# A tangent computed by an exponential and three VectorE steps in the first router of a fused decoder layer

## The reference

```python
pooled = x.mean(axis=1)
h = jnp.tanh(pooled @ W1 + b1)            # 64 values
logits = h @ W2 + b2                      # 8 experts
probs = jax.nn.softmax(logits, axis=-1)
top_p, top_i = jax.lax.top_k(probs, 3)    # top_w = top_p / sum
# x + sum over the three experts of  w * (gelu(x @ Wa[e]) @ Wb[e])
```

## Time and profile before

| | us |
|---|---|
| median of 3 runs | 1166.26 |
| lowest, highest | 1164.23, 1167.35 |
| the profiled execution | 1166.95 |
| its span, first to last instruction | 1165.2 |
| TensorE busy | 1112.1 (95%) |
| VectorE busy | 896.5 (77%) |
| ScalarE busy | 815.4 (70%) |
| GpSimd busy | 576.3 (49%) |
| mean granted TensorE clock | 0.986 of full |

### The profile page before, as it was taken

How to read it: one execution, slowest core, us unless ns; L and a number is a source line. 1 busy time by engine, 2 the same in 40 slices (tenths; PEclk the granted TensorE clock), 3 DMA queues, 4 the chain that set the end, 5 groups by cost and what they waited for, 6 DMA issues and landing times.

```text
span 1165.2 us, 24724 instructions
## 1 busy us (share of the span) xinstructions
PE 1112.1 (95%) x8375; PEld 516.4 (44%) x8375; DVE 896.5 (77%) x2816; ACT 815.4 (70%) x1553; POOL 576.3 (49%) x594
## 2 busy tenths in 40 slices
PE   7799999999999999978999999999989999999998
PEld 3344444444444444335422223233223676666666
DVE  4678888888788878875999988998975768565654
ACT  5467767766666666654588897887886867657563
POOL 2878888888888888856324344443312130000000
PEclk9899999999999999998999999999998999999999
DMA  7744333343333333104223131221205324234200
GB/s 215 212 131 120 88 111 88 87 120 82 84 91 85 86 86 86 51 1 113 57 58 83 57 83 55 74 65 48 64 1 188 103 73 145 91 106 130 73 19 19
DMA packets 81859, 102.86 MB, mean 88 GB/s; under 512 B 11875, under 2 KB 73571, under 8 KB 81735
## 3 DMA queue, kind: packets, MB, share of 16 engines
q1 hardware_dynamic: 81574, 100.90, 29.9%
q10 hardware_dynamic: 160, 0.39, 0.2%
HBM read 65.27 MB, written 10.68 MB: 65 GB/s over the span
## 4 chain that ended last, share of the span: by engine, by line
PE 40%; DVE 6%; ACT 5%; issue 4%; ACTq 0%
PE a_s L1534 11%; PE a_m L1520 7%; PE a_o L1453 7%; PE a_m L1403 4%; DVE a_mx L1875 3%; PE a_s L1433 3%; PE a_a L169 3%; PE a_s L1520 2%; ACT a_pt L1678 2%; PE a_s L169 1%; PE a_a L1461 1%; ACT a_osb L1684 1%; PE a_m L1478 0%; DVE a_mx L1872 0%; ACT a_back L1690 0%
## 5 line engine op out<-in xcount | busy, mean ns | idle before, releaser
L1678 ACT ACTIVATE a_pt<-a_s 128x512 f32<-128x512 f32 (+1 forms) x448 | 228.8, 574 | 50.5 <-PE a_s L1433 47.7
L739 ACT ACTIVATE a_pt<-a_s 128x512 f32<-128x512 f32 x256 | 152.9, 598 | 130.0 <-DVE a_s L893 126.1
L1875 DVE TENSOR_REDUCE a_mx<-a_m 128x1 f32<-128x512 f32 x256 | 163.0, 683 | 21.0 <-PE a_m L1403 20.2
L884 DVE CUSTOM_DVE_ANT_0 a_junk<-a_m,a_rtile 128x512 f16<-128x512 f32 x256 | 167.2, 686 | 0.5 <-issue 0.5
L996 POOL TENSOR_TENSOR a_ps<-a_ps,a_pt 128x512 f32<-128x512 f32 x126 | 159.8, 1290 | 3.2 <-ACT a_pt L739 3.1
L893 DVE TENSOR_TENSOR a_s<-a_s,a_near 128x218 f32<-128x218 f32 (+1 forms) x256 | 108.0, 432 | 41.8 <-PE a_s L527 41.8
L538 PE MATMUL a_o<-a_pt,a_v 128*64 128x512 f32 x512 | 124.0, 605 | 0.0
L1872 DVE CUSTOM_DVE_ANT_0 a_junk<-a_m,a_causal 128x512 f16<-128x512 f32 (+3 forms) x256 | 113.8, 486 | 6.2 <-issue 5.8
L526 PE MATMUL a_s<-a_q,a_k 128*128 128x512 f16 x256 | 98.5, 385 | 5.7 <-ACT a_pt L739 5.6
L1008 POOL TENSOR_TENSOR x_acc<-x_acc,a_part 128x256 f32<-128x256 f32 x120 | 87.3, 728 | 27.2 <-DVE x_acc L916 26.4
L527 PE MATMUL a_s<-a_q,a_k 74*128 74x512 f16 x256 | 98.5, 385 | 0.0
(11 more groups left out here) (328 smaller groups left out, 2633.6 us busy)
## 6 DMA issues: line engine op xcount, KB each, us to landing
a_rtile<-lines SPq DMA_DIRECT2D x32, 448.0 KB, 3.9
a_q<-a_nat SPq DMA_DIRECT2D x192, 64.0 KB
a_k<-a_nat SPq DMA_DIRECT2D x192, 64.0 KB
a_vy<-in_Wa SPq DMA_DIRECT2D x12, 1024.0 KB, 5.0
a_vy<-in_Wb SPq DMA_DIRECT2D x12, 1024.0 KB, 7.5
a_qk<-halves SPq DMA_DIRECT2D x40, 128.0 KB, 2.8
halves<-a_held SPq DMA_DIRECT2D x16, 256.0 KB, 2.2
halves<-a_held SPq DMA_DIRECT2D x32, 128.0 KB, 2.4
```

Source lines behind the costliest of these rows:

```text
L739: act.activation(pt[:, n % RING, ::-1], bank_s[j % 2][:, :], ACT.Exp, scale=SC1 / QS).then_inc(sm["act_s"], 1)
L884: dve.tensor_tensor_reduce(junk[h][:, :], bank_m[h][:, :], rtile[:, u % 3, h, qb * P:qb * P + S], -1 / MAXROW, 3e38, ALU.add, ALU.min, mx[ ...
L1678: act.activation(to, frm, ACT.Exp, scale=SC2 / QS).then_inc(sm["act_s"], 1)
L1875: dve.tensor_reduce(mx[u % 2][:, qb, to:to + 1], frm, AX.X, ALU.max).then_inc(sm["dve_b"], 1)
```

## The change

In the router of batches 0 and 1 the Tanh is replaced by tanh(z) = 1 - 2 / (exp(2z) + 1). VectorE adds the bias and bounds z at 40 (`bounded`, step 240), ScalarE takes exp(2z) (step 241, where Tanh stood at the end of step 240), and VectorE adds 1, inverts, and multiplies by -2 and adds 1 into `ht` (`tangent`, step 241). The second product moves from step 241 to 243 on TensorE, with the VectorE and ScalarE parts behind it from step 242 to 244, the spread from 245 to 246, and `wbc` and `chosen` from 246 to 247. The router of batches 2 and 3 keeps its Tanh.

```diff
-        rt = semaphores(nc, ctx, "rt", "ld one pe act v")
+        rt = semaphores(nc, ctx, "rt", "ld one pe act v tangent")
+        hz, he = sb("hz", [RH, 2]), sb("he", [RH, 2])
-        POOLED, FIRST, SECOND, SPREAD, SPLIT0, UP0 = 236, 240, 241, 245, 254, 265
+        POOLED, FIRST, SECOND, SPREAD, SPLIT0, UP0 = 236, 240, 243, 246, 254, 265
@@ TensorE, route, part 1
                     pe.wait_ge(rt["act"], 3 * r + 2)
+                    if r == 0:
+                        pe.wait_ge(rt["tangent"], 4)
@@ ScalarE, route
+                elif part == 1 and r == 0:
+                    act.wait_ge(rt["tangent"], 1)
+                    act.activation(he[:, :], hz[:, :], ACT.Exp, scale=2.0).then_inc(rt["act"], 1)
                 elif part == 1:
                     act.wait_ge(rt["pe"], 3 * r + 1)
-                    if r == 0:
-                        act.wait_ge(rt["ld"], len(loads) * DMA)
@@ ScalarE, clock
-                for i, at in enumerate((POOLED, FIRST, SECOND + 1)):
+                for i, at in enumerate((POOLED, FIRST + 1, SECOND + 1)):
@@ VectorE
+            def bounded(frm):
+                dve.wait_ge(rt["pe"], 1)
+                dve.wait_ge(rt["ld"], len(loads) * DMA)
+                dve.tensor_scalar(hz[:, :], frm[0:RH, 16:18], b1[:, :], 40.0, ALU.add, ALU.min).then_inc(rt["tangent"], 1)
+            def tangent():
+                dve.wait_ge(rt["act"], 2)
+                dve.tensor_scalar(he[:, :], he[:, :], 1.0, None, ALU.add).then_inc(rt["tangent"], 1)
+                dve.wait_ge(rt["tangent"], 2)
+                dve.reciprocal(hz[:, :], he[:, :]).then_inc(rt["tangent"], 1)
+                dve.wait_ge(rt["tangent"], 3)
+                dve.tensor_scalar(ht[0:RH, 0:2], hz[:, :], -2.0, 1.0, ALU.mult, ALU.add).then_inc(rt["tangent"], 1)
@@ VectorE, clock
+                if n == FIRST:
+                    bounded(bank_m[0])
+                if n == FIRST + 1:
+                    tangent()
```

## The result

| | before | after |
|---|---|---|
| median | 1166.68 us (11 runs) | 1162.58 us (11 runs) |
| lowest, highest | 1164.23, 1167.48 | 1160.67, 1164.27 |
| span of the profiled execution | 1165.2 | 1162.1 |
| mean granted clock in it | 0.986 | 0.992 |

The ratio of after to before is 0.997, with a 95% interval of 0.996 to 0.9981: the changed kernel is 4.1 us faster in the medians. 1161.6 us was forecast.

What follows compares the result with a forecast made beforehand. TensorE, busy 95%, was taken to bound the kernel, losing time to a 1.36 us gap and the half-speed clock behind it. Removing 4.7 us (1.36 - 0.5 gap, 3.8 clock) from 1166.26 gave 1161.6 us, range 1159.5 to 1166.0.

Steps and rivals of the forecast that it cites:

- TensorE's gain of 4.7 us in the tail: From 868.6 us to the products with values behind the spread: 1.36 - 0.5 of gap plus 3.8 of clock.
- its slack: Choice of experts ends near 878.2 on VectorE, TensorE reaches the spread at 879.0: 0.8 us, so no wait.
- The four steps: VectorE's bound, add, invert and multiply-add: 0.2 us each, the first hidden, the other three 0.6 us before the second product.
- No table load: The Exp replacing Tanh on ScalarE needs no load, so the Tanh's load of 1.28 us goes.
- The drain: The skill adds about 1.38 us to ScalarE's 1.28 us load; the prediction expected no such drain to be saved.
- The slack behind the experts' weights: Last transposition waiting for `weigh_last`: 3.7 us of slack shrinks to 0.7 us, so the gain is narrowly not capped.
- 1.7 us earlier: Experts' loads issued once `chosen` ends, at 880.0 against 881.76: 1.7 us earlier, while TensorE comes 4.7 us earlier.
- Does the clock hold: Clock stays 1.00 around 870 us because the fall looks narrow and about 0.9 us leaves the gap; 3.8 us rests on it.
- the table load stays: Rival: the load stays ahead of the new Exp and stalls a score bank, gap 1.1 us; 1166 us, chance 0.03.
- the wait moves to the spread: Rival: VectorE's chain ends late, TensorE waits 1.4 us at step 246, clock falls; 1167.5 us, up to 1170, chance 0.08.

Runs made afterwards that it cites:

- the gap filled over 128 rows: Kernel before with six idle products over all 128 rows on TensorE ahead of the second product; 1166.3 us, and 1165.33 us when run again.
- the kernel with the load forced back: Changed kernel with a table load (exp_and_others) forced ahead of the new exponential; 1166.97 us, ratio 0.9998.
- the move alone: Kernel before with the second product at step 243 and the spread at 246, Tanh and its table load kept; 1166.97 us, ratio 1.0.
- the kernel with the long gap and no load: Changed kernel with second product at step 241, spread at 245, ScalarE's exponential still at the end of step 241; 1167.74 us, ratio 1.0.
- idle products over 64 rows: Kernel before with six idle products (64x128 weights, 512 columns) on TensorE ahead of the second product; 1164.71 us, ratio 0.9992.

## Why the prediction was right, point by point

- **TensorE's gain of 4.7 us in the tail**: measured 4.78 (16.99 - 12.21), and 281.22 us behind it in both. The profiles of another kernel agree with the split: the gap filled over 128 rows gives 3.66 us for the clock (forecast 3.8), and the rest, 4.78 - 3.66 = 1.1, is the gap's (0.9). The medians of that kernel, 0.6 and 1.5 us below the kernel before, do not confirm it.
- **Positions**, each less the 1.68 us of different start: tangent ready 870.60 (forecast 870.8), choice of experts 878.05 (878.2), spread 878.89 (879.0), its slack 0.84 (0.8), `chosen` 879.70 (880.0).
- **The four steps**: 0.16 to 0.21 us each, 0.2 from one start to the next, as taken. The new Exp: 0.20.
- **No table load**: right. From 560 to 900 us the preload is the only one left:

```profile
L1772 ACT ACT_TABLE_LOAD x1 | 1.3, 1283 | 0.0
```

- **The drain** that the Trainium skill, "ScalarE: Activation LUTs", section "What ACT_TABLE_LOAD costs", adds to the load: not seen. Where the load was forced back, it started 0.02 us after the exponentials ahead of it ended (871.54, 871.56), and the next activation came 1.30 us after its start.
- **The slack behind the experts' weights** was mis-sized: forecast 0.7 us, measured 2.4 (`weigh_last` ends at 898.79, the transposition starts at 901.21). Its term "1.7 us earlier" is 3.5 after the different start (900.63 - 898.79 + 1.68): `chosen` is 0.3 us earlier than I had it, from there to the first split it takes 6.36 us against 7.08, and the four pairs of splits take 7.9 us against 8.6. The error was on the safe side.

```profile
887.74 0.69 DVE L2006 TENSOR_SCALAR a_cx<-a_vy 128x1024 f16<-128x1024 f32 x1 [3.33 <-DMA a_vy<-in_Wa]
...
895.51 0.34 DVE L1900 RECIPROCAL a_r<-a_back 128x32 f32<-128x32 f32 x1
...
898.37 0.42 DVE L1893 TENSOR_TENSOR a_ys<-a_a,a_r 128x256 f32<-128x256 f32 x1
...
901.21 0.60 PE L1462 MATMUL a_a<-ident,a_osb 128*128 128x128 f32 x4
```

- **Does the clock hold**: yes, in both profiles of the changed kernel. The argument for it, that the fall is narrow and the gap decides, holds for gaps of 1.4 and 2.1 us. A gap of 1.20 us in the same tail passed at 1.00. It does not hold for everything: a fall came behind gaps of 0.45 and 0.18 us in one kernel, and behind one of 0.88 in another. The changed kernel keeps gaps of 0.67 and 0.19 us. That these kept the clock is seen in four profiles (both of this kernel, and both kernels with the second product at 242), but no row says that they must.
- **The rival "the table load stays"** was priced at 1166: the kernel with the load forced back gave 1166.97. The price agrees in part by luck, since the rival put the fall at the load, and in the profile the clock held there (stretch 13.39 us) and fell 12 us behind it. The rival "the wait moves to the spread" did not come true here, by 0.84 us; with the second product at 242 and the spread at 245 it does, at 1.20 us, though without the fall that the rival had priced for a wait of 1.4.
- **The median** was forecast 1.0 us too low. Of this, 0.4 us is the starting point: the sum began at 1166.26, the median of three executions, and that of eleven is 1166.68. The other 0.6 us is the gain, 4.1 in the medians against 4.7. The likely reason is that the sum counts the whole price of the fall for every execution, while by the mean clocks the kernel before pays it in part of them only.

## What to carry to other kernels

When TensorE's granted clock falls in a profile, look for the idle time ahead of the fall, then for what the *other* engine did in it: here a table load of 1.28 us for a tangent of 64 by 2 values cost over four. Replacing a function by one of the loaded set removed the stall here; moving its consumer only moved the wait, as the move alone showed. And measure a small change by a stretch between two fixed instructions, which repeated within 0.04 us here, beside a median over executions that scatter by several microseconds.

## What the runs showed of the hardware

- Mean clocks of the unchanged kernel lie between 0.983 and 0.992 from one execution to the next. Its two profiles show the same fall behind the same gap (1.36 and 1.37 us), so that the fall is shorter or missing in some executions is read from the means alone.
- Length alone does not decide: in the tail the clock fell behind gaps of 1.36, 1.37, 2.11 and 2.12 us and not behind one of 1.20; elsewhere it passed 1.24 us at 1.00, and fell once behind 0.88 us.
- The fall can come late: in the kernel with the long gap and no load the gap ended at 873.63 us, and the clock was still 1.00 from 874 to 875.
- TensorE busy with idle products over 64 rows did not keep the clock in one profile (0.50 for about three microseconds); over 128 rows it did in two. What decides stays open.
